# First attention phase of a fused graph and expert network: score products of 512 columns with s rows placed by transfers, the mean folded into the head weights, values made in halves

## The reference, cut to what matters

```python
x = x + _L0_gnn_ref(_layernorm(x), adj, adj[None], W, a_src, a_dst, beta_tilde, W_out)

def _L0_gnn_ref(x, adj, prior, W, a_src, a_dst, beta_tilde, W_out):
    x_proj = jnp.einsum('bnd,hdf->bhnf', x, W)            # 8 heads of 16 channels
    e_src = jnp.einsum('bhnf,hf->bhn', x_proj, a_src)     # s
    e_dst = jnp.einsum('bhnf,hf->bhn', x_proj, a_dst)     # d
    e = jax.nn.leaky_relu(e_src[..., :, None] + e_dst[..., None, :], 0.2)
    e = e + (softplus(beta_tilde) * jnp.log(prior + 1e-6))[:, None, :, :]
    e = jnp.where(adj[None, None, :, :] > 0, e, neg_inf)
    attn = jax.nn.softmax(e, axis=-1)
    h = jnp.einsum('bhij,bhjf->bhif', attn, x_proj)
    return h.transpose(0, 2, 1, 3).reshape(B, N, D) @ W_out.T
```

## Time and profile before

| what | value |
|---|---|
| median of 3 runs | 1065.49 us |
| the 3 runs | 1058.89, 1073.07, 1065.49 us |
| profiled execution: span, first to last instruction | 1059.3 us |
| its setup, up to the first instruction of the attention phase | 18.8 us |
| its first attention, up to the first instruction of the experts phase | 18.8 to 278.8 us |
| busy in the whole span: PE, DVE, ACT, POOL | 927.0, 717.5, 661.1, 504.2 us |

### The profile page before, as it was taken

One profiled execution on the slowest core, in us unless ns is written; L12 is line 12 of the kernel. 1 busy time (PEld: TensorE's weight loads), 2 busy tenths in 40 slices (PEclk: granted clock), 3 DMA queues, 4 the chain that ended last, 5 costly groups with the idle time before them and its releaser, 6 DMA issues. The chain is left out here.

```text
span 1059.3 us, 25141 instructions
## 1 busy us (share of the span) xinstructions
PE 927.0 (88%) x8021; PEld 805.6 (76%) x8021; DVE 717.5 (68%) x2252; ACT 661.1 (62%) x1691; POOL 504.2 (48%) x498
## 2 busy tenths in 40 slices
PE   1799998999899999999998994798898888768997
PEld 1588887887688999999998993466565666548896
DVE  4599888988464135555554544579898888678775
ACT  4556665654544546666665662688888888867652
POOL 2566564663035564444444442576767732244340
PEclk9999998999699999999999996999999999978999
DMA  7913221211354216777676861011111100000112
GB/s 195 371 50 122 120 109 70 114 42 54 101 148 131 65 49 194 212 202 197 198 200 173 210 162 33 23 33 34 32 35 28 35 6 1 1 1 20 41 42 60
DMA packets 93007, 103.59 MB, mean 98 GB/s; under 512 B 16352, under 2 KB 69856, under 8 KB 90720
## 3 DMA queue, kind: packets, MB, share of 16 engines
q1 hardware_dynamic: 73232, 59.78, 17.3%
q10 hardware_dynamic: 11472, 25.63, 9.0%
q0 software_dynamic: 8192, 16.79, 5.5%
HBM read 52.60 MB, written 43.27 MB: 91 GB/s over the span
## 5 line engine op out<-in xcount | busy, mean ns | idle before, releaser
L1319 POOL DMA_INDIRECT slot_rows_in<-xn_all,slots x128 | 130.1, 1016 | 142.7 <-DMA slot_rows_in<-xn_all,slots 105.8
L1205 ACT ACTIVATE s_hT<-s_hp,expert 128x256 f32<-128x256 f32 x284 | 111.5, 476 | 52.4 <-PE s_hp L1196 52.4
L1218 PE MATMUL s_yp<-w_experts,s_hT 128*128 x1136 | 138.0, 275 | 0.0
L1218 PEld LDWEIGHTS s_yp<-w_experts,s_hT 128*128 128x128 f32 x1136 | 132.8, 192 | 0.0
L1226 DVE TENSOR_TENSOR xnT_all<-s_yp,expert 128x256 f32<-128x256 f32 x71 | 30.2, 425 | 117.9 <-PE s_yp L1218 114.7
L489 DVE SCALAR_TENSOR_TENSOR l_mi<-l_sbc,mT 128x512 bf16<-128x512 f32 x128 | 84.3, 668 | 4.0 <-PE l_sbc L480 3.3
L1194 PE MATMUL s_hp<-e_xh,e_wh 128*128 128x256 f32 x284 | 85.9, 303 | 0.0
L1196 PE MATMUL s_hp<-e_xh,e_wl 128*128 128x256 f32 x284 | 80.1, 282 | 0.0
L1195 PE MATMUL s_hp<-e_xl,e_wh 128*128 128x256 f32 x284 | 80.1, 282 | 0.0
L1176 ACT CAST e_wh<-expert 128x512 fp32r<-128x512 f32 x71 | 43.9, 619 | 48.8 <-issue 43.1
L1120 ACT ACTIVATE s_hT<-s_hp,b_shared 128x512 f32<-128x512 f32 x64 | 42.8, 688 | 48.4 <-PE s_hp L1091 47.2
(11 more groups left out here) (353 smaller groups left out, 2701.0 us busy)
## 6 DMA issues: line engine op xcount, KB each, us to landing
expert<-expert_rows ACTq DMA_DIRECT2D x65, 322.0 KB, 3.4
slot_rows_in<-zeros SPq DMA_DIRECT2D x9, 1024.0 KB, 12.2
...
slot_rows_out<-zeros SPq DMA_DIRECT2D x8, 1024.0 KB, 4.4
xn_all<-l_xr SPq DMA_DIRECT2D x16, 256.0 KB, 2.3
xnT_all<-l_rT SPq DMA_DIRECT2D x16, 256.0 KB
out_dram<-xn_all SPq DMA_DIRECT2D x16, 256.0 KB, 2.3
```

Of the source, the lines that this page charges most:

```text
L1205: nc.scalar.activation(hT[q % 2][:, c, :], hp[:, c, 0:TILE], ACT.Gelu, bias=wt[q][:, F + c:F + c + 1]).then_inc(s["h_ok"], 1)
L1218: ins = pe.matmul(yp[q % 2][:, h * D:(h + 1) * D], hT[q % 2][:, c, h * P:(h + 1) * P], w2, start=(c == 0 and h == 0), stop=(c == FC - 1), ...
L1319: pool.indirect_dma_start(k.rows_in, bass.IndirectOffsetOnAxis(ap=k.slots[:, c, b:b + 1], axis=0), k.xn[:, b, :], None).then_inc(scattered ...
```

## The change

1. Scores: one product of 512 columns for each batch and half, in place of one of 512 and four of 128. It contracts only the 32 rows of the batch: 16 high and 16 low bfloat16 parts of s and d. Its moving operand `blocks` holds, for each head, the s rows of that head in their own block of 128 columns, and zeros and ones elsewhere. The s rows are put there by 8 transfers per group on SyncE's queue (`sp_y_blocks`), each 8 rows of 256 bytes.
2. For that the low parts are made before the transpose (`pool_y_low`, GpSimd), so `pe_y_transpose` has a second, bfloat16 product, and ScalarE makes two copies (`act_y_parts`) where it made one.
3. The mean is taken out of the head weights in setup (a 144-column product and one VectorE instruction), so that stage n needs no shift: L350 is gone. L585 becomes two GpSimd instructions at the end of its slot.
4. `dve_y_small` has two instructions in place of four; ScalarE makes three exponentials in place of one; the minimum with 1 is taken in `dve_z_post`.
5. Scaling, remainders and casts of the values are done in two halves of 16 head rows each.
6. Setup: no selector tables; the loads of x quarters 1 to 3 are issued by SyncE behind the weights. The zeros for `slot_rows_in` are spread, one transfer per group, and those for `slot_rows_out` follow them.

The core of the diff:

```diff
+                for q in range(1, 4):
+                    sp.dma_start(k.x[:, 16 * q:16 * q + 16, :],
+                                 a["x"][16 * q:16 * q + 16].rearrange("b t d -> t b d")).then_inc(k.x_loaded[q], 16)
...
-                nc.scalar.copy(k.sel_s[:], diag_s[:].unsqueeze(2).to_broadcast([P, HB, P]))
...
-                dve.tensor_copy(k.sel_d[:], diag_d[:].unsqueeze(2).to_broadcast([P, HB, P]))
+                dve.wait_ge(pool_made, 2)
+                dve.tensor_copy(k.ident16[:], k.ident[:])
...
+                for p in range(2):
+                    dve.tensor_copy(k.blocks[p][:], d_heads[:].unsqueeze(2).to_broadcast([P, HEADS, P]))
...
+                chain(dve.scalar_tensor_tensor(k.w_heads[:], tr[:, 3, 0:D + 16], -1.0 / D, k.w_heads[:],
+                                               ALU.mult, ALU.add))
...
+                pe.matmul(tr[:, 3, 0:D + 16], k.ones[:], k.w_heads[:], start=True, stop=True).then_inc(pe_t, 1)
...
-        def dve_x_shift(dve, g, p):
-            wait(dve, s["rstd_ok"], g + 1)
-            dve.scalar_tensor_tensor(shift[p][:], mv[p][:, :, 0], -1.0, rstd[p][:], ALU.mult, ALU.mult)\
-                .then_inc(s["shift_ok"], 1)
         def act_x_apply(act, g, p):
             wait(act, s["xT_ps"], g)
-            wait(act, s["shift_ok"], g + 1)
-            nc.scalar.copy(act_fence[:], shift[p][:, 0:1])
+            wait(act, s["rstd_ok"], g + 1)
+            nc.scalar.copy(act_fence[:], rstd[p][:, 0:1])
...
         def act_x_scores(act, g, p):
             wait(act, s["vs_ps"], g + 1)
             wait(act, s["pk_ok"], g - 1)
+            nc.scalar.copy(sd[p][:].rearrange("p k b h -> p b k h"),
+                           four[:, :, D:D + 16].rearrange("p b (k h) -> p b k h", k=2)).then_inc(s["sd_ok"], 1)
+            wait(act, s["t_ps"], g)
+            nc.scalar.copy(sd16[:, :, 0, :], four[:, :, D:D + 16]).then_inc(s["s_hi"], 1)
...
+        def act_x_values(act, g, p):
+            wait(act, s["vb_ok"], 2 * (g - 1))
+            wait(act, s["pv_ps"], (g - 1) * GB)
+            nc.scalar.copy(k.v17[p][:, :, 0:DH].rearrange("p (b h) f -> p b h f", b=GB),
+                           four[:, :, 0:D].rearrange("p b (h f) -> p b h f", h=HEADS)).then_inc(s["vs_ok"], 1)
+        def pool_y_low(pool, g, p):
+            wait(pool, s["sd_ok"], g + 1)
+            wait(pool, s["s_hi"], g + 1)
+            pool.tensor_tensor(sd16[:, :, 1, :].rearrange("p b (k h) -> p b k h", k=2),
+                               sd[p][:].rearrange("p k b h -> p b k h"),
+                               sd16[:, :, 0, :].rearrange("p b (k h) -> p b k h", k=2), ALU.subtract)\
+                .then_inc(s["s_lo"], 1)
...
         def pe_y_transpose(pe, g, p):
             wait(pe, s["sd_ok"], g + 1)
-            pe.transpose(cc[:, 0:P], sd[p][:].rearrange("p k b h -> p (k b h)"), k.ident[:]).then_inc(s["t_ps"], 1)
-        def act_y_hi(act, g, p):
+            pe.transpose(cc[0:HB, 256:256 + P], sd[p][:, 1].rearrange("p b h -> p (b h)"), k.ident[:])
+            wait(pe, s["s_lo"], g + 1)
+            pe.matmul(cc[:, 0:P], sd16[:].rearrange("p b t c -> p (b t c)"), k.ident16[:], start=True, stop=True)\
+                .then_inc(s["t_ps"], 1)
+        def act_y_parts(act, g, p):
             wait(act, s["t_ps"], g + 1)
+            wait(act, s["blocks_ok"], 16 * HEADS * g)
+            nc.scalar.copy(sparts[:], cc[:, 0:P]).then_inc(s["sparts_ok"], 1)
             wait(act, s["s_ps"], (g - 1) * 2 * GB)
-            nc.scalar.copy(sparts[p][:], cc[:, 0:P]).then_inc(s["hi_ok"], 1)
+            nc.scalar.activation(dparts[p][:], cc[:, 0:P], ACT.Identity, scale=k.is_d[:], bias=k.is_s[:])\
+                .then_inc(s["dparts_ok"], 1)
+        def sp_y_blocks(sp, g, p):
+            wait(sp, s["sparts_ok"], g + 1)
+            wait(sp, s["s_ps"], (g - 1) * 2 * GB)
+            for h in range(HEADS):
+                sp.dma_start(k.blocks[p][h:P:16, h, :], sparts[h:P:16, :]).then_inc(s["blocks_ok"], 16)
         def dve_y_max(dve, g, p):
-            wait(dve, s["hi_ok"], g + 1)
+            wait(dve, s["dparts_ok"], g + 1)
             wait(dve, s["dm_ps"], g)
-            dve.tensor_reduce(dmax[32:64, :], cc[32:64, 0:P], AX.X, ALU.max).then_inc(s["dg_self"], 1)
-            dve.tensor_tensor(sparts[p][64:128, :], cc[64:128, 0:P], sparts[p][64:128, :], ALU.subtract)\
-                .then_inc(s["sp_ok"], 1)
+            dve.tensor_reduce(dmax[0:HB, :], cc[0:HB, 256:256 + P], AX.X, ALU.max).then_inc(s["dg_self"], 1)
             wait(dve, s["dg_self"], g + 1)
-            dve.tensor_scalar(dmdiag[32:64, :], k.diag32[32:64, :], dmax[32:64, :], None, ALU.mult)\
+            dve.tensor_scalar(dmdiag[0:HB, :], k.ident[0:HB, 0:HB], dmax[0:HB, :], None, ALU.mult)\
                 .then_inc(s["diag_ok"], 1)
...
-            dve.tensor_tensor(us[:], cc[:, P:P + HB], s_i, ALU.add).then_inc(s["us_self"], 1)
-            wait(dve, s["us_self"], g + 1)
-            dve.tensor_scalar(pk[p][:, 1], pk[p][:, 0], 0.2, None, ALU.mult)
-            dve.tensor_scalar(pk[p][:, 2], us[:], -0.8, 0.0, ALU.mult, ALU.min).then_inc(s["pk_ok"], 1)
+            dve.tensor_tensor(pk[p][:, 1], cc[:, P:P + HB], s_i, ALU.add).then_inc(s["pk_ok"], 1)
         def act_y_exp(act, g, p):
             wait(act, s["pk_ok"], g + 1)
             wait(act, s["heads_ok"], (g - 1) * GB)
-            nc.scalar.activation(bdg[p][:], pk[p][:], ACT.Exp).then_inc(s["bdg_ok"], 1)
-        def pool_y_scale(pool, g, p):
+            nc.scalar.activation(bdg[p][:, 0], pk[p][:, 0], ACT.Exp)
+            nc.scalar.activation(bdg[p][:, 1], pk[p][:, 0], ACT.Exp, scale=0.2).then_inc(s["bdg_ok"], 1)
+            nc.scalar.activation(bdg[p][:, 2], pk[p][:, 1], ACT.Exp, scale=-0.8).then_inc(s["row_exp"], 1)
...
+        half_rows = [slice(HB // 2 * o, HB // 2 * o + HB // 2) for o in range(2)]
+        def pool_y_scale(pool, g, p, o):
+            rows = half_rows[o]
...
+            wait(pool, s["vs_ok"], g + 1)
+            wait(pool, s["vh_ok"], 2 * (g - 1) + o + 1)
+        def act_y_vhi(act, g, p, o):
+            rows = half_rows[o]
+            wait(act, s["vp_ok"], 2 * g + o + 1)
             wait(act, s["pv_ps"], (g - 1) * GB)
...
         def pe_z_scores(pe, g, p, b):
             if b == 0:
-                wait(pe, s["sp_ok"], g + 1)
+                wait(pe, s["blocks_ok"], 16 * HEADS * (g + 1))
+                wait(pe, s["dparts_ok"], g + 1)
+            rows = slice(32 * b, 32 * b + 32)
             for h in range(2):
                 wait(pe, s["mi_ok"], g * 2 * GB + 2 * b + h - 1)
-                pe.matmul(sbc[:, h, :].rearrange("p (q i) -> p q i", q=4), sparts[p][:], k.sel_d[:, c:c + 4, :],
-                          start=True, stop=False, skip_group_check=True)
-                for q in range(4):
-                    ins = pe.matmul(sbc[:, h, q * P:(q + 1) * P], k.sel_s[:, c + q, :], sparts[p][:],
-                                    start=False, stop=(q == 3), skip_group_check=True)
-                ins.then_inc(s["s_ps"], 1)
+                pe.matmul(sbc[:, h, :].rearrange("p (q i) -> p q i", q=4), dparts[p][rows, :],
+                          k.blocks[p][rows, 4 * h:4 * h + 4, :], start=True, stop=True).then_inc(s["s_ps"], 1)
...
-            dve.tensor_tensor(leaked[b % 2][:], out[:, :, VW:2 * VW],
-                              bdg[p][:, 2, rows].unsqueeze(2).to_broadcast([P, HEADS, VW]), ALU.mult)\
+            dve.scalar_tensor_tensor(leaked[b % 2][:], bdg[p][:, 2, rows].unsqueeze(2).to_broadcast([P, HEADS, VW]),
+                                     1.0, out[:, :, VW:2 * VW], ALU.min, ALU.mult)\
...
-        def dve_r_shift(dve, g):
-            wait(dve, s["rstd_r"], g + 1)
-            dve.scalar_tensor_tensor(shift_r[:], mv_r[:, :, 0], -1.0, rstd_r[:], ALU.mult, ALU.mult)\
-                .then_inc(s["shift_r"], 1)
+        def pool_r_shift(pool, g):
+            wait(pool, s["rstd_r"], g + 1)
+            pool.tensor_tensor(neg_mean_r[:], k.zeros[:, 0:GB], mv_r[:, :, 0], ALU.subtract).then_inc(s["neg_mean_r"], 1)
+            wait(pool, s["neg_mean_r"], g + 1)
+            pool.tensor_tensor(shift_r[:], neg_mean_r[:], rstd_r[:], ALU.mult).then_inc(s["shift_r"], 1)
...
                 act_x_scores(act, g + 1, q)
-                act_y_hi(act, g + 1, q)
                 act_x_values(act, g + 1, q)
+                act_y_parts(act, g + 1, q)
             if on["l"]:
                 act_r_apply(act, g - 3)
             if on["y"]:
                 act_y_exp(act, g + 1, q)
             if on["x"]:
                 act_x_xT(act, g + 2, p)
+            if on["y"]:
+                act_y_vhi(act, g + 1, q, 0)
             if on["l"]:
                 act_l_rT(act, g - 3)
             if on["y"]:
-                act_y_vhi(act, g + 1, q)
+                act_y_vhi(act, g + 1, q, 1)
             if on["r"]:
                 act_r_rstd(act, g - 2)
             if on["n"]:
                 act_x_rstd(act, g + 3, q)
+            if on["y"]:
```

(22 more changed lines are left out.)

162 lines of the change are left out of this document (70 added, 92 removed).

## The result

The changed kernel takes 1095.7 us (median), against 1063.8 for the kernel before on the same chip: ratio 1.029, 95% interval 1.020 to 1.038. It is slower by some 32 us, where the forecast was 1040 us and a gain; whether it is slower by 2%, the interval leaves open. The profiled execution has a span of 1102.8 us at a mean granted clock of 0.908 (before: 1059.3 at 0.962).

A forecast was written before the change was run, and what follows sets the result against it. The prediction took a loop through four engines to set the clean slot of the first attention. Gains of 12.95 (eleven slot intervals), 5.8 (start) and 0.5 (rest) make 19.3: from 1059.3 to 1040.0 us, own range 1033 to 1048.

The forecast's parts named there:

- the clean slot stays at 13.5: First attention: a slot without stalls, A, B and C in turn, takes 13.48 us after 13.55 before.
- rival 3: TensorE's clock falls more often, with a longer pause before the maxima product: 4 x 2.5 us, total 1050; chance 0.15.
- A: Slot's first stretch, VectorE working without a pause up to the statistics: 7.28 us, from 7.81.
- B: Slot's second stretch, from the statistics through ScalarE's hT copy and TensorE's projection to the next scores: 3.42 us, from 2.87.
- C: Slot's third stretch, from the scores through the transpose and ScalarE's copies to the maximum of d: 2.78 us, from 2.87.
- The stalls of the shifts: VectorE's shifts held up beside GpSimd subtractions in the first attention, with clock falls behind some: all 12.4 us go.
- Half cast 0.55: In B, ScalarE's cast of half the middle parts now stands ahead of the hT copy: 0.55 us more per slot.
- Rival 4: GpSimd's loop is longer and TensorE stands still at the transpose: slot 14.4 us, total 1050; chance 0.13.
- Rival 2: The small block transfers land late and the scores wait: 5.0 us a slot, total 1110; chance 0.12.
- The three short slots: First attention's slots from 40.21 to 78.07, without stalls: no change, 0 us.
- Start: Setup and start: attention begins at 12.8 instead of 18.8; the maximum of group 1 comes 5.8 us sooner.
- Everything else: Short slots 0, last two score slots -1.5, GpSimd's shift in the tail +1.0: sum -0.5 us.

The follow-up runs named there:

- e5_128_rows: Changed kernel with each score product over all 128 rows instead of its batch's 32, so scores are sums over four batches: ratio 0.985 to the kernel before.
- e3_before_one_product: Kernel before without the four s products of each score half, so the s term is missing from the scores: ratio 0.989 to the kernel before.
- e9_padded: Changed kernel with score products over 128 rows, 96 of them zeros, the zeroed tile written by four ScalarE activations instead of one: ratio 1.019 to the kernel before.
- e13_padded_by_transfer: Changed kernel with score products over 128 rows, 96 of them zeros, the zeroed tile filled by four more SyncE transfers: ratio 0.987 to the kernel before.
- e4_before_no_shifts: Kernel before with the mean folded into the head weights, no shift in stage n, the other shift on GpSimd: ratio 0.993 to the kernel before.

## Why the prediction was wrong

**The step that failed** is "the clean slot stays at 13.5", in the place where it takes the full clock over from the earlier trace rows; the prediction named the mechanism as rival 3 ("the clock falls more often") with a chance of 0.15 and a price of "4 x 2.5". It falls in every slot from the fourth mark (65.81) on, not in one of three, and costs 3.4 us in each (17.0 against the 13.57 of e5_128_rows), 42.7 us by the attention's end (309.7 against 267.0), where the rival had 10. The rival's price per fall, 2.5, was low but of the right size; how often it falls was not. I had tied the fall to the length of the pause (0.7 then, about 1.2 to come). The pause came as forecast (1.07), but e3_before_one_product and e5_128_rows have the same one at the full clock. What matters is what TensorE is given around it: score products over 32 rows instead of 128. The prediction counted these by their durations, and they have the same duration. That the rows decide is shown by one edit in either direction; how rows and idle time act together on the clock is not.

I named the rule of the Trainium skill there ("TensorE: Matmul & The Clock Gate", A second HAM failure mode: small idles between groups of products let the clock swing). The swing is in the trace (0.50 for 10.2 us of 17.1), and so is a lower clock with longer pauses at 128 rows (0.94 in e9_padded, 0.98 in e13_padded_by_transfer); as the whole cause the rule doesn't hold here, since a pause of 1.15 us leaves the clock at 1.00 with 128 rows.

The same page (Why this matters for your kernels) says that a product over 32 rows takes as long as one over 128, and advises to put small ones in separate row groups so that they run at the same time. The first half is what the rows above show (0.60 and 0.59 us a pair). The second is not used here: the row groups differ by batch, but one batch's pair starts at 147.04 and the next one's at 151.91. What few rows do to the clock the page doesn't say; here they cost 4%.

**The other steps**, read where the clock holds:
- The slot. e5_128_rows from 131.98: A 7.20, B 3.63, C 2.71, together 13.54, where 7.28, 3.42 and 2.78 made 13.48. The loop through four engines was right, and so was that the saved scores buy nothing in a clean slot.
- The stalls of the shifts, 12.4 us: gone; 10.6 measured alone in e4_before_no_shifts, at the attention's end. The eleven intervals from the fifth mark take 149.4 us in e5_128_rows against 161.45, 12.1 less, where the sum had 12.95. The diagonal (L420, now L424), which the prediction named as the next candidate for such a stall, takes 0.23 us in all 16 slots.
- Half cast 0.55: 0.54. That "one half of it stands between" costs the loop held, but against whole values it was a gain, since the low part on GpSimd is new as well. Rival 4's place was right for that variant alone.
- Block transfers at no cost: right. 0.61 us an issue instead of 0.47, 4.85 in all, inside the slack. Rival 2 is out.
- The three short slots from the second mark to the fifth, put at 0: they take 44.9 us instead of 37.9, and 42.0 in e5_128_rows. So the whole gain of the start is gone by the fifth mark (80.44; 77.65 in e5_128_rows; 78.07 before). In the changed kernel pairs of score products still take 1.03 us up to 54.56, so TensorE is at half clock there, although the clock column reads 1.00 from 35.59 to 65.81; in this early part only the durations show it. In the kernel before, the products are at their full-clock time from 44.07 on (0.38 us, 0.63 before that).
- Start: the attention was to begin at 12.8 and begins at 15.14; the second mark gains 4.6 instead of 5.8. VectorE's chain in setup waits for a load until 11.69 and ends at 14.40; I had it end near 12:

```profile
11.69 0.42 DVE L221 TENSOR_TENSOR wa_prod<-w_heads,a_heads 128x256 f32<-128x256 f32 x1 [1.94 <-DMA a_heads<-in_L_gnn_a_dst_dram]
...
14.31 0.09 DVE L234 MEMSET v<- 128x32 f32 x1
```

- Everything else: no stage's code changed, yet the span behind the attention was 780.5 us before, 793.1 in the changed kernel, and 773.7 to 803.4 in the fifteen others. By the chips it is 787.6 to 799.9, 773.7 to 786.4, 794.5 to 803.4 and 776.1 to 779.9 us in the four groups, and the first and third are also those where the kernel before is slower (1072.5 and 1070.5). So a part of it goes with the chip; the 12.6 us between the two kernels on one chip stay open.

With the clock held the forecast would have been nearer, though not all of it for the right reason: e5_128_rows at 1046.0 and e13_padded_by_transfer at 1050.0 are 16.8 and 11.1 us below the kernel before, where 19.3 was the sum, but at the attention's end, which is all that the sum is about, they gain 11.8 and 11.0. Most of the rest is the start's 5.8, of which 0.4 is left at the fifth mark of e5_128_rows.

Not tried: a longer pause by itself at 128 rows (e9_padded changes it with ScalarE's work), a pause shortened by itself at 32 rows, and 128 rows in the maxima product, which also has 32.
